# Handing the experts' output banks from TensorE to VectorE in two halves instead of one

## The chip, the core and the metric

The kernel runs on one core of a Trainium2 chip. The metric is the device time of one execution in microseconds. It is compared as the median of several runs.

## The reference

The kernel computes one hybrid block on eight images of 192 channels and 1,024 positions: a spiking convolution-attention part, causal softmax attention with six heads, and a mixture of four experts of which each token uses two. The change touches the last part alone. In the reference it is this:

```python
scores = jnp.einsum('bsd,de->bse', x, gate_w) + gate_b
probs = jax.nn.softmax(scores, axis=-1)
topk_vals, topk_idx = jax.lax.top_k(probs, TOP_K)
...
h = jax.nn.gelu(jnp.einsum('bsd,edh->ebsh', x, w1) + b1[:, None, None, :], approximate=False)
y = jnp.einsum('ebsh,ehd->ebsd', h, w2) + b2[:, None, None, :]
out = jnp.einsum('bse,ebsd->bsd', masked, y)
```

All four experts are computed for all tokens. The gate is zero where an expert isn't chosen.

## The kernel before

An image has 1,024 tokens, in two blocks of 512 (`NB = 2`), and a block has four tiles of 128 tokens (`TB = 4`). An expert's hidden layer of 768 is cut into six chunks of 128 (`HC = 6`), so a block has 24 chunks and an image 48. The order of the work on each engine is written out by hand: every engine has its own program, and semaphores join them.

For chunk `i` of an image the steps are:

- TensorE, `hidden(i)`: five matmuls of 512 columns (L437) make the chunk's hidden values in bank 0 or 1 of PSUM.
- ScalarE: GELU (L874), then the f16 high part (L882). VectorE: the f16 low part (L1330).
- TensorE, `expert_out(i - 3)` (L708): three chunks later, twelve matmuls of 192 columns, three for each of four tiles, add the chunk's share to the expert's output. Tiles 0 and 1 lie in bank 2 of PSUM and tiles 2 and 3 in bank 3. Behind the last chunk of an expert each tile gets one matmul more, for the bias (L713), and the sixteenth matmul raises `f2_done`.
- VectorE, `add_expert(y)` (L1314): once an expert is complete, four instructions multiply the four tiles by the gate and add them to `acc`. The fourth raises `y_used`.
- TensorE may write the first chunk of the next expert only when `y_used` has been raised, since there is one set of output banks.

Between these steps TensorE, ScalarE and VectorE take pieces of the next image's front part (`following`) and of this image's own tail (`aside`), at places fixed by tables (`FRONT_AT`, `TAIL_AT`). The front part ends with row maxima of the attention scores: matmuls (L596, L600) whose results VectorE reduces (L1148). The tail holds `ul` (L1192), the low part of block 1's expert input, and the front holds `al` (L1131), the same for the attention input. TensorE waits for both. The eighth image has no `following`. At the end ScalarE starts the store of `acc`, when `y_used` has its last count.

In `experts` on VectorE, `add_expert` stands ahead of the low part of chunk `i`, so that everything behind it on VectorE waits as long as it waits.

Of the kernel before, what the change touches and what calls it, by code (L numbers as in the profile page):

```python
# [10 lines left out]
ALU = mybir.AluOpType  # L11
# [4 lines left out]
B, C, N = 8, 192, 1024  # L16
# [4 lines left out]
NB = N // QB  # L21
TB = QB // P
# [5 lines left out]
EXPERTS, HID = 4, 4 * C  # L28
HC = HID // P
# [103 lines left out]
def build(nc, x_ch, x_tok, consts, w_conv, bn, w_in, w_out, b1, b2, gate_b, out):  # L133
    with ExitStack() as ctx:
        def sb(name, shape, dt):
            return ctx.enter_context(nc.sbuf_tensor(name, shape, dt))
# [3 lines left out]
        def sem(name, gain=0):  # L140
            handle = ctx.enter_context(nc.semaphore(name))
            per_image[handle.name] = gain
            return handle

        def at(s, img, n):

            return img * per_image[s.name] + n
# [38 lines left out]
        acc = sb("acc", [P, NT, C], F32)  # L186
# [23 lines left out]
        half = 4 * 2 * QB  # L210
# [48 lines left out]
        gate = sb("gate", [P, NT, EXPERTS], F32)  # L259
# [11 lines left out]
        ps = ctx.enter_context(nc.psum_tensor("ps", [P, 8, QB], F32))  # L271
# [78 lines left out]
        h_hi = sem("h_hi", NB * CHUNKS)  # L350
        h_lo = sem("h_lo", NB * CHUNKS)
        f2_done = sem("f2_done", NB * CHUNKS)
        y_used = sem("y_used", NB * EXPERTS)
        stored = sem("stored", 16 * NB)


# [71 lines left out]
        def _(pe):  # L428
            def project(dst, high, low, cols, tok, tokens_stationary):


                for n, (w, a, c) in enumerate(((win_h, high, 0), (win_l, high, 0), (win_h, low, 0),
                                               (win_t, high, 1), (win_t, low, 1))):
                    lhs, rhs = w[:, cols], a[:, c, tok]
                    if tokens_stationary:
                        lhs, rhs = rhs, lhs
                    mm = pe.matmul(dst, lhs, rhs, start=(n == 0), stop=(n == 4))  # L437
                return mm
# [234 lines left out]
            def experts(img, following):  # L673

                def hidden(i):
                    b, n = divmod(i, CHUNKS)

                    if i == 0:
                        pe.wait_ge(o_done, at(o_done, img, NB * PAIRS - 1))
                    elif i == 1:  # L680
                        pe.wait_ge(e_done, at(e_done, img, NE))
                    elif i == 3:
                        pe.wait_ge(o_done, at(o_done, img, NB * PAIRS))
                    if i >= 2:
                        pe.wait_ge(h_act, at(h_act, img, i - 1))
                    if n == 0:
                        pe.wait_ge(ul_done, at(ul_done, img, b + 1))
                    col = COL_W1 + n * P
                    project(ps[:, H_BANK[i], :], uh, ul, slice(col, col + P), slice(b * QB, (b + 1) * QB), False)\
                        .then_inc(h_ps, 1)  # L690

                def expert_out(i):
                    b, n = divmod(i, CHUNKS)
                    e, k = divmod(n, HC)
                    if k == 0:

                        if i == 0:
                            pe.wait_ge(gate_used, at(gate_used, img, 1))
                        else:
                            pe.wait_ge(y_used, at(y_used, img, i // HC))  # L700
                    pe.wait_ge(h_lo, at(h_lo, img, i + 1))
                    s = i % N_H
                    for t in range(TB):
                        dst = ps[:, 2 + t // 2, (t % 2) * C:(t % 2 + 1) * C]
                        tok = slice(t * P, (t + 1) * P)
                        for m, (hid, w) in enumerate(((h_h, wout_h), (h_h, wout_l), (h_l, wout_h))):

                            mm = pe.matmul(dst, hid[:, s, tok], w[:, n, :],  # L708
                                           start=(k == 0 and m == 0 and t % 2 == 0), stop=False,
                                           skip_group_check=True)  # L710
                        if k == HC - 1:

                            mm = pe.matmul(dst, b2_ones[:, :], b2_sb[:, e * C:(e + 1) * C],  # L713
                                           start=False, stop=True, skip_group_check=True)
                    mm.then_inc(f2_done, 1)

                aside = Aside(tail(img, 1, True))
                for i in range(NB * CHUNKS + F_LAG):
                    if i < NB * CHUNKS:
                        hidden(i)  # L720
                    following.until(i - 0.5)
                    if i >= F_LAG and (i - F_LAG) % HC == 0:

                        aside.until(i)
                        following.until(i)
                    if i >= F_LAG:
                        expert_out(i - F_LAG)
                    aside.until(i)
                    following.until(i)
                following.finish()  # L730
# [5 lines left out]
            for what, n in ((bn_t[:, 2, :], 0), (bn_t[:, 3, :], 1)):  # L736
                for p in range(3):
                    for c in range(2):
                        mm = pe.transpose(ps[0:CC + 1, p, n * C + c * CC:n * C + (c + 1) * CC],
                                          what[:, 4 * c + 1 + p:4 * c + 2 + p].broadcast_to([CC, CC + 1]),  # L740
                                          ident[0:CC, 0:CC])
# [16 lines left out]
        def _(act):  # L758
# [56 lines left out]
                rows_of_maxima(img, 0, 4)  # L815

            def store(img, b):
                act.wait_ge(y_used, at(y_used, img, (b + 1) * EXPERTS))
                act.dma_start(out[img, :, b * TB:(b + 1) * TB, :], acc[:, b * TB:(b + 1) * TB, :])\
                   .then_inc(stored, 16)  # L820

# [88 lines left out]
            for img in range(B - 1):  # L910
                experts(img, Aside(front(img + 1, True)))
                attend(img + 1, img)
            experts(B - 1, Aside(iter(())))
            store(B - 1, 1)
            act.wait_ge(stored, B * whole(stored))

# [66 lines left out]
        def _(dve):  # L983
            V = nc.vector
# [320 lines left out]
            def experts(img, following):  # L1305
                def add_expert(y):

                    b, e = divmod(y, EXPERTS)
                    dve.wait_ge(f2_done, at(f2_done, img, (y + 1) * HC))
                    for t in range(TB):  # L1310
                        n = b * TB + t
                        if y and t == 0:
                            dve.wait_ge(y_used, at(y_used, img, y))
                        ins = V.scalar_tensor_tensor(  # L1314
                            out=acc[:, n, :], in0=ps[:, 2 + t // 2, (t % 2) * C:(t % 2 + 1) * C],
                            scalar=gate[:, n, e:e + 1], in1=acc[:, n, :], op0=ALU.mult, op1=ALU.add)
                    ins.then_inc(y_used, 1)

                aside = Aside(tail(img, 1, True))
                for i in range(NB * CHUNKS + F_LAG):  # L1320
                    following.until(i - 0.5)
                    if i >= F_LAG and (i - F_LAG) % HC == HC - 1:
                        add_expert((i - F_LAG) // HC)
                    if i < NB * CHUNKS:
                        if i >= N_H:

                            dve.wait_ge(f2_done, at(f2_done, img, i - N_H + 1))
                        s = i % N_H
                        dve.wait_ge(h_hi, at(h_hi, img, i + 1))
                        V.scalar_tensor_tensor(out=h_l[:, s, :], in0=h32[:, s, :], scalar=A_SCALE,  # L1330
                                               in1=h_h[:, s, :], op0=ALU.mult, op1=ALU.subtract)\
                         .then_inc(h_lo, 1)
                    aside.until(i)
                    following.until(i)
                following.finish()
# [34 lines left out]
            for c in range(2):  # L1370
                three = wc[0:CC, c, C:].rearrange("p (k n) -> p k n", k=3)
                step(V.scalar_tensor_tensor(out=three, in0=three, scalar=W_SCALE, in1=ps[0:CC, 0:3, 0:C],
                                            op0=ALU.mult, op1=ALU.mult))
# [11 lines left out]
            for n, (kind, c0, w) in enumerate(pieces):  # L1385
# [5 lines left out]
                                       op0=ALU.mult, op1=ALU.subtract).then_inc(stage_lo, 1)  # L1391
# [79 lines left out]
```

## Time and profile before

| | before |
|---|---|
| median of 3 runs | 1701.42 us (1701.23 to 1702.93) |
| the profiled execution: its own time | 1703.11 us |
| the profiled execution: span of its instructions | 1701.1 us |
| TensorE, matmuls busy | 1590.3 us, 93% of the span |
| VectorE busy | 1188.9 us, 70% |
| ScalarE busy | 904.1 us, 53% |
| mean granted TensorE clock | 0.976 of full speed |

Busy times are sums over instructions, and the matmuls of TensorE overlap one another in them. An engine's idle time costs something only where another engine on the path to the end waits for it. The profile's names: PE is TensorE's matmul, PEld its weight load, DVE VectorE, ACT ScalarE. `L708` is line 708 of the kernel.

### The profile page before, as it was taken

How to read it: one execution, taken by the hardware profiler on the slowest of the kernel's cores; microseconds unless marked ns; L12 is line 12 of the kernel's file. 1: busy time of each engine (PE TensorE's matmuls, PEld its weight loads, DVE VectorE, ACT ScalarE, POOL GpSimd, SP SyncE). 2: the span in 40 equal slices, each digit the busy share in tenths (PEclk: the TensorE clock that was granted, in tenths of full speed). 3: DMA queues.
4: the chain of work that ended last, by engine and by line, in shares of the span. 5: the costliest groups of instructions: out<-in, count | busy, mean ns of one | idle time of the engine just before them, and what ended most of it. 6: DMA issues, size and time to landing. Idle time of an engine off the chain costs nothing.

```text
span 1701.1 us, 32601 instructions
## 1 busy us (share of the span) xinstructions
PE 1590.3 (93%) x13148; PEld 1028.3 (60%) x13148; DVE 1188.9 (70%) x2537; ACT 904.1 (53%) x1329; POOL 173.3 (10%) x247
## 2 busy tenths in 40 slices
PE   3689999999999999899998999999999999999998
PEld 1424676546665567656765567655766557665666
DVE  6685775767767676867759578576776777686643
ACT  3206654466545665456553665446654566535654
POOL 2210102001110003000120010200121000300100
PEclk9759999999999999999999999999999999999999
DMA  4112002010111002010020100201011100200000
GB/s 158 52 29 63 1 1 66 8 41 2 26 41 48 1 1 66 2 48 1 2 66 1 48 2 1 66 13 36 2 38 30 48 2 1 66 1 11 1 11 10
DMA packets 25129, 47.27 MB, mean 28 GB/s; under 512 B 7410, under 2 KB 16946, under 8 KB 23700
## 3 DMA queue, kind: packets, MB, share of 16 engines
q1 hardware_dynamic: 15728, 27.85, 5.9%
q0 software_dynamic: 6144, 9.45, 2.4%
q10 hardware_dynamic: 3108, 7.91, 1.3%
q8 instruction: 103, 1.69, 0.4%
q14 instruction: 46, 0.38, 0.1%
HBM read 19.82 MB, written 6.29 MB: 15 GB/s over the span
## 4 chain that ended last, share of the span: by engine, by line
PE 67%; DVE 23%; ACT 4%; issue 3%; POOL 1%; DMA 1%; SPq 0%; DVEq 0%; ACTq 0%; POOLq 0%
PE ps L437 20%; PE ps L708 16%; PE ps L655 10%; DVE mx L1148 7%; PE ps L472 6%; PE ps L596 3%; DVE acc L1314 3%; DVE room L1330 3%; PE ps L516 2%; DVE norm_stats L989 2%; PE ps L444 1%; PE ps L503 1%; ACT room L874 1%; PE ps L476 1%; DVE gn_st L1031 1%
## 5 line engine op out<-in xcount | busy, mean ns | idle before, releaser
L874 ACT ACTIVATE room<-ps,b_sb 128x512 f32<-128x512 f32 x384 | 263.2, 685 | 459.8 <-PE ps L437 459.8
L708 PE MATMUL ps<-wout_h,room 128*128 128x192 f16 x3072 | 459.4, 246 | 5.4 <-DVE acc L1314 5.4
L1330 DVE SCALAR_TENSOR_TENSOR room<-room 128x512 f16<-128x512 f32 x384 | 262.7, 687 | 179.2 <-ACT room L882 174.2
L708 PE MATMUL ps<-wout_l,room 128*128 128x192 f16 x1536 | 377.9, 246 | 0.0
L708 PEld LDWEIGHTS ps<-wout_h,room 128*128 128x128 f16 x3072 | 286.5, 98 | 45.7 <-DVE acc L1314 11.8
L854 ACT ACTIVATE room<-ps 128x1024 f32<-128x1024 f32 (+3 forms) x288 | 224.8, 811 | 161.0 <-PE ps L476 123.6
L1148 DVE TENSOR_REDUCE mx<-ps 128x2 f32<-128x1024 f32 (+3 forms) x288 | 265.8, 952 | 36.3 <-PE ps L600 19.2
L882 ACT ACTIVATE room<-room 128x512 f16<-128x512 f32 x384 | 241.9, 630 | 33.8 <-ACT room L874 0.4
L655 PE MATMUL ps<-room,v 128*64 128x512 f32 (+3 forms) x1152 | 232.9, 488 | 0.9 <-DVE o L1280 0.9
L596 PE MATMUL ps<-qk 96*128 96x512 f16 (+3 forms) x576 | 159.8, 349 | 38.7 <-DVE mx L1148 30.3
L708 PEld LDWEIGHTS ps<-wout_l,room 128*128 128x128 f16 x1536 | 150.4, 98 | 27.3
L472 PE MATMUL ps<-qk 98*64 98x512 f16 (+3 forms) x1152 | 157.1, 332 | 10.2 <-DVE mx L1148 7.8
L437 PE MATMUL ps<-uh,win_h 128*128 128x512 f16 x384 | 145.9, 380 | 3.0 <-DVE o L1280 3.0
L437 PE MATMUL ps<-uh,win_t 128*128 128x512 f16 x384 | 145.7, 380 | 0.0
L437 PE MATMUL ps<-ul,win_h 128*128 128x512 f16 x384 | 145.7, 379 | 0.0
L437 PE MATMUL ps<-uh,win_l 128*128 128x512 f16 x384 | 145.6, 379 | 0.0
L437 PE MATMUL ps<-ul,win_t 128*128 128x512 f16 x384 | 145.5, 379 | 0.0
L1314 DVE SCALAR_TENSOR_TENSOR acc<-ps,gate,acc 128x192 f32<-128x192 f32 x256 | 89.0, 410 | 72.4 <-PE ps L713 71.7
L472 PEld LDWEIGHTS ps<-qk 98*64 98x64 f16 x1152 | 62.2, 110 | 93.4 <-issue 47.5
L596 PEld LDWEIGHTS ps<-qk 96*128 96x128 f16 x576 | 53.7, 100 | 106.2 <-DVE mx L1148 61.5
L961 POOL TENSOR_TENSOR norm_pow<-norm_var,minus_half 128x4 f32<-128x4 f32 x16 | 18.6, 1165 | 916.7 <-DVE norm_var L1003 916.7
L655 PEld LDWEIGHTS ps<-room,v 128*64 128x64 f32 x1152 | 66.5, 137 | 30.0 <-issue 3.0
(201 smaller groups left out, 2291.0 us busy)
## 6 DMA issues: line engine op xcount, KB each, us to landing
xc<-x_ch SPq DMA_DIRECT2D x8, 768.0 KB, 5.7
qk<-qk_all SPq DMA_DIRECT2D x96, 64.0 KB, 2.4
qk<-qk_all POOLq DMA_DIRECT2D x96, 64.0 KB, 2.6
out<-acc ACTq DMA_DIRECT2D x16, 384.0 KB, 2.4
xt<-x_tok SPq DMA_DIRECT2D x7, 768.0 KB, 7.0
qk<-qk_all POOLq DMA_DIRECT2D x96, 32.0 KB, 2.0
qk<-qk_all SPq DMA_DIRECT2D x96, 32.0 KB, 2.3
room<-w_in SPq DMA_DIRECT2D x2, 1024.0 KB, 8.5
```

The costliest lines, as they stand in the source:

```text
L437: mm = pe.matmul(dst, lhs, rhs, start=(n == 0), stop=(n == 4))
L472: mm = pe.matmul(ps[keys, bank, q0:QB], k4[:, h, kc * P + keys.start:kc * P + keys.stop], q4[:, h, b * QB + q0:(b + 1) * QB], start=True, ...
L516: mm = pe.matmul(ps[:, 4 + (t + 2) % 4, 0:2 * C], xs[0:rows, c, t * P:(t + 1) * P], w[0:rows, c, C:3 * C], start=(n == 0), stop=(n == 3))
L596: mm = pe.matmul(ps[:, bank, 0:width], q4[0:3 * D, h, t * P:(t + 1) * P], k4[0:3 * D, h, half * QB:half * QB + width], start=True, stop=no ...
L655: mm = pe.matmul(ps[a * 2 * D:(a + 1) * 2 * D, bank, q0:QB], v32[:, kc * PAIRS + pair, a * D:(a + 2) * D], p32[j % N_P32][:, a, q0:QB], st ...
L708: mm = pe.matmul(dst, hid[:, s, tok], w[:, n, :], start=(k == 0 and m == 0 and t % 2 == 0), stop=False, skip_group_check=True)
L854: act.activation(p32[j % N_P32][:, :, q0:QB], ps[:, bank:bank + 2, q0:QB], ACT.Exp, scale=scale).then_inc(e_done, 1)
L874: act.activation(h32[:, i % N_H, :], ps[:, H_BANK[i], :], ACT.Gelu, scale=1 / (U_SCALE * W_SCALE), bias=b1_sb[:, n:n + 1])\
L882: act.activation(h_h[:, i % N_H, :], h32[:, i % N_H, :], ACT.Copy, scale=A_SCALE)\
L1148: V.tensor_reduce(mx[:, half, t, 2 * pair:2 * pair + 2], ps[:, bank:bank + 2, 0:width], AX.X, ALU.max)\
L1314: ins = V.scalar_tensor_tensor(out=acc[:, n, :], in0=ps[:, 2 + t // 2, (t % 2) * C:(t % 2 + 1) * C], scalar=gate[:, n, e:e + 1], in1=acc[: ...
L1330: V.scalar_tensor_tensor(out=h_l[:, s, :], in0=h32[:, s, :], scalar=A_SCALE, in1=h_h[:, s, :], op0=ALU.mult, op1=ALU.subtract)\
```

## The change

The one hand-over of four tiles becomes two of two tiles, one for each bank. TensorE raises a new semaphore `y_half` with the bias matmul of tile 1. VectorE's adds of tiles 0 and 1 wait for `y_half`, and those of tiles 2 and 3 for `f2_done`. `y_used` counts twice for an expert, and TensorE waits for it twice: before tile 0 and before tile 2 of the next expert's first chunk. The store of `acc` waits for the doubled count.

```diff
         f2_done = sem("f2_done", NB * CHUNKS)
-        y_used = sem("y_used", NB * EXPERTS)
+        y_half = sem("y_half", NB * EXPERTS)
+        y_used = sem("y_used", 2 * NB * EXPERTS)
...
                         else:
-                            pe.wait_ge(y_used, at(y_used, img, i // HC))
+                            pe.wait_ge(y_used, at(y_used, img, 2 * (i // HC) - 1))
                     pe.wait_ge(h_lo, at(h_lo, img, i + 1))
                     s = i % N_H
                     for t in range(TB):
+                        if k == 0 and i and t == TB // 2:
+                            pe.wait_ge(y_used, at(y_used, img, 2 * (i // HC)))
...
                             mm = pe.matmul(dst, b2_ones[:, :], b2_sb[:, e * C:(e + 1) * C],
                                            start=False, stop=True, skip_group_check=True)
+                            if t == TB // 2 - 1:
+                                mm.then_inc(y_half, 1)
                     mm.then_inc(f2_done, 1)
...
-                act.wait_ge(y_used, at(y_used, img, (b + 1) * EXPERTS))
+                act.wait_ge(y_used, at(y_used, img, 2 * (b + 1) * EXPERTS))
...
-                    dve.wait_ge(f2_done, at(f2_done, img, (y + 1) * HC))
-                    for t in range(TB):
-                        n = b * TB + t
-                        if y and t == 0:
-                            dve.wait_ge(y_used, at(y_used, img, y))
-                        ins = V.scalar_tensor_tensor(
-                            out=acc[:, n, :], in0=ps[:, 2 + t // 2, (t % 2) * C:(t % 2 + 1) * C],
-                            scalar=gate[:, n, e:e + 1], in1=acc[:, n, :], op0=ALU.mult, op1=ALU.add)
-                    ins.then_inc(y_used, 1)
+                    for half in range(2):
+
+                        if half == 0:
+                            dve.wait_ge(y_half, at(y_half, img, y + 1))
+                        else:
+                            dve.wait_ge(f2_done, at(f2_done, img, (y + 1) * HC))
+                        if y:
+                            dve.wait_ge(y_used, at(y_used, img, 2 * y - 1 + half))
+                        for t in range(half * TB // 2, (half + 1) * TB // 2):
+                            n = b * TB + t
+                            ins = V.scalar_tensor_tensor(
+                                out=acc[:, n, :], in0=ps[:, 2 + t // 2, (t % 2) * C:(t % 2 + 1) * C],
+                                scalar=gate[:, n, e:e + 1], in1=acc[:, n, :], op0=ALU.mult, op1=ALU.add)
+                        ins.then_inc(y_used, 1)
```

No instruction changes its place. What changes is who waits for what. On TensorE, in the eighth image, the last boundary between two experts read like this before; `b_sb,b_ones` is the bias matmul of a tile, `uh,win_h` the first matmul of `hidden`, and `room` holds the hidden values:

```order
10278 L713 MATMUL ps<-b_sb,b_ones 128x192
10279 L437 MATMUL ps<-uh,win_h 128x512 [waits h_act]
10280 L437 MATMUL ps<-uh,win_l 128x512
10281 L437 MATMUL ps<-ul,win_h 128x512
10282 L437 MATMUL ps<-uh,win_t 128x512
10283 L437 MATMUL ps<-ul,win_t 128x512
10284 L708 MATMUL ps<-wout_h,room 128x192 [waits h_lo,y_used]
10285 L708 MATMUL ps<-wout_l,room 128x192
10286 L708 MATMUL ps<-wout_h,room 128x192 x2
10287 L708 MATMUL ps<-wout_l,room 128x192
10288 L708 MATMUL ps<-wout_h,room 128x192 x2
```

At the same place TensorE's program now reads as follows (the line numbers have moved by one and by three):

```order
10333 L716 MATMUL ps<-b_sb,b_ones 128x192
10334 L438 MATMUL ps<-uh,win_h 128x512 [waits h_act]
10335 L438 MATMUL ps<-uh,win_l 128x512
10336 L438 MATMUL ps<-ul,win_h 128x512
10337 L438 MATMUL ps<-uh,win_t 128x512
10338 L438 MATMUL ps<-ul,win_t 128x512
10339 L711 MATMUL ps<-wout_h,room 128x192 [waits h_lo,y_used]
10340 L711 MATMUL ps<-wout_l,room 128x192
10341 L711 MATMUL ps<-wout_h,room 128x192 x2
10342 L711 MATMUL ps<-wout_l,room 128x192
10343 L711 MATMUL ps<-wout_h,room 128x192
10344 L711 MATMUL ps<-wout_h,room 128x192 [waits y_used]
```

Nothing stands elsewhere; a second wait for `y_used` has come between tile 1 and tile 2. On VectorE, from the second-last add to the end of the program, the order before was this (`room<-room` is the low part of a chunk):

```order
1922 L1314 SCALAR_TENSOR_TENSOR acc<-ps,gate,acc 128x192 [waits y_used,f2_done]
1923 L1314 SCALAR_TENSOR_TENSOR acc<-ps,gate,acc 128x192 x3
1924 L1330 SCALAR_TENSOR_TENSOR room<-room 128x512 [waits h_hi,f2_done] x4
1925 L1314 SCALAR_TENSOR_TENSOR acc<-ps,gate,acc 128x192 [waits y_used,f2_done]
1926 L1314 SCALAR_TENSOR_TENSOR acc<-ps,gate,acc 128x192 x3
```

And now it is this, for the same stretch of VectorE:

```order
2046 L1324 SCALAR_TENSOR_TENSOR acc<-ps,gate,acc 128x192 [waits y_used,y_half]
2047 L1324 SCALAR_TENSOR_TENSOR acc<-ps,gate,acc 128x192
2048 L1324 SCALAR_TENSOR_TENSOR acc<-ps,gate,acc 128x192 [waits y_used,f2_done]
2049 L1324 SCALAR_TENSOR_TENSOR acc<-ps,gate,acc 128x192
2050 L1340 SCALAR_TENSOR_TENSOR room<-room 128x512 [waits h_hi,f2_done] x4
2051 L1324 SCALAR_TENSOR_TENSOR acc<-ps,gate,acc 128x192 [waits y_used,y_half]
2052 L1324 SCALAR_TENSOR_TENSOR acc<-ps,gate,acc 128x192
2053 L1324 SCALAR_TENSOR_TENSOR acc<-ps,gate,acc 128x192 [waits y_used,f2_done]
```

The four adds of an expert stay together; the first now waits for `y_half`, and the third for `f2_done`.

## Rows read from the trace of the kernel before

**Rows 1.** The page: its first line, and the chain that ended last, by engine.

```profile
span 1701.1 us, 32601 instructions
...
PE 67%; DVE 23%; ACT 4%; issue 3%; POOL 1%; DMA 1%; SPq 0%; DVEq 0%; ACTq 0%; POOLq 0%
```

**Rows 2.** Waits, whole span: who waited for whom, us in total, times, longest.

```profile
DVE acc L1314 <- PE ps L713: 71.7, 43, 3.1
...
PEld ps L472 <- issue: 47.5, 186, 0.8
...
PEld ps L596 <- issue: 18.5, 30, 1.4
...
PEld ps L708 <- DVE acc L1314: 11.8, 13, 1.0
...
PE ps L708 <- DVE acc L1314: 5.4, 13, 0.5
```

**Rows 3.** Timeline, fourth image, around its fifth expert: start us, duration us.

```profile
879.74 0.25 PE L713 MATMUL ps<-b_sb,b_ones 128*128 128x192 f16 x1
...
880.40 0.25 PE L713 MATMUL ps<-b_sb,b_ones 128*128 128x192 f16 x1
...
880.69 1.39 DVE L1314 SCALAR_TENSOR_TENSOR acc<-ps,gate,acc 128x192 f32<-128x192 f32 x4 [2.84 <-PE ps L713]
...
881.35 0.38 PE L437 MATMUL ps<-ul,win_t 128*128 128x512 f16 x1
...
882.00 0.68 DVE L1330 SCALAR_TENSOR_TENSOR room<-room 128x512 f16<-128x512 f32 x1
...
882.14 0.26 PE L708 MATMUL ps<-wout_h,room 128*128 128x192 f16 x1 [0.41 <-DVE acc L1314]
```

**Rows 4.** Timeline, eighth image: from one chunk's hidden values to the next expert_out.

```profile
1663.53 0.38 PE L437 MATMUL ps<-ul,win_t 128*128 128x512 f16 x1
...
1663.75 0.25 PE L708 MATMUL ps<-wout_h,room 128*128 128x192 f16 x1
```

**Rows 5.** Timeline, eighth image, the adds of the last expert.

```profile
1696.97 1.39 DVE L1314 SCALAR_TENSOR_TENSOR acc<-ps,gate,acc 128x192 f32<-128x192 f32 x4 [2.09 <-PE ps L713]
```

**Rows 6.** Timeline, fourth image, from its first expert to the gate scores.

```profile
800.34 0.69 DVE L1330 SCALAR_TENSOR_TENSOR room<-room 128x512 f16<-128x512 f32 x1
...
800.78 0.25 PE L713 MATMUL ps<-b_sb,b_ones 128*128 128x192 f16 x1
...
801.73 1.39 DVE L1314 SCALAR_TENSOR_TENSOR acc<-ps,gate,acc 128x192 f32<-128x192 f32 x4 [0.69 <-PE ps L713]
...
804.15 1.00 ACT L826 ACTIVATE uh<-ps 128x1024 f16<-128x1024 f32 x1
...
805.57 1.21 DVE L1192 SCALAR_TENSOR_TENSOR ul<-ps,uh 128x1024 f16<-128x1024 f32 x1
...
806.46 0.25 PE L708 MATMUL ps<-wout_h,room 128*128 128x192 f16 x1
...
806.84 0.18 PE L437 MATMUL ps<-win_h,uh 128*128 128x4 f16 x1
```

**Rows 7.** Line 1192 (`ul`), all instructions: who waited for it, us, times.

```profile
  PEld ps L437: 2.5, 7
```

**Rows 8.** Timeline, fourth image, around its fourth expert.

```profile
858.01 1.39 DVE L1314 SCALAR_TENSOR_TENSOR acc<-ps,gate,acc 128x192 f32<-128x192 f32 x4 [1.02 <-PE ps L713]
...
860.83 0.38 PE L437 MATMUL ps<-al,win_t 128*128 128x512 f16 x1
...
861.19 0.39 PE L437 MATMUL ps<-ah,win_h 128*128 128x512 f16 x1
```

**Rows 9.** Timeline, fourth image, VectorE in the row maxima.

```profile
894.46 3.07 DVE L1148 TENSOR_REDUCE mx<-ps 128x2 f32<-128x768 f32 x3
897.62 1.39 DVE L1314 SCALAR_TENSOR_TENSOR acc<-ps,gate,acc 128x192 f32<-128x192 f32 x4
...
921.36 1.38 DVE L1314 SCALAR_TENSOR_TENSOR acc<-ps,gate,acc 128x192 f32<-128x192 f32 x4
```

## The prediction

> **What bounds the kernel now.** I read the page first: the span is 1701.1 us, and the chain of work that ended last runs over TensorE for 67% of it and over VectorE for 23% [rows 1]. So I ask where TensorE stands still and who ends it. That is the list of waits. Its two rows on the changed lines say that the first matmul of an expert's first chunk (L708) stood still for the adds (L1314) 13 times, and no more [rows 2]. An image has seven boundaries between experts, eight images have 56; the other 43 are covered by front or tail work. The other direction is longer: VectorE sat idle for the end of an expert 43 times, 71.7 us in all [rows 2]. That costs something only where TensorE later waits for what stands behind the adds on VectorE. So I went through one whole image on the timeline, with its TensorE gaps, and then saw that the other images have the same ones.
>
> The kind of stop to see first is at the fifth expert [rows 3]. The last bias matmul starts at 880.40, VectorE begins the four adds at 880.69, `hidden` is through with its last start at 881.35, and the next expert's first matmul starts only at 882.14. Six of the 13 stops are of the eighth image, which has no front work to cover them, one is in each of the other seven.
>
> **The change part by part.** Lengths first. Four adds take 1.39 us, and the instruction behind them starts 1.31 us after the first [rows 3]: one add holds VectorE for 0.33 us and its result is there after 0.41. From a bias matmul's start to the first add's start is 0.29 us (880.40 to 880.69), and from the end of the adds (882.08) to the matmul that waited is 0.06. The bias matmul of tile 1 stands 0.66 us ahead of that of tile 3 (879.74, 880.40) [rows 3]. So `y_half` lets the adds of tiles 0 and 1 start up to 0.66 us sooner, they take 0.66 us, and the adds of tiles 2 and 3 then go at the old start of all four. VectorE is free 0.65 us sooner wherever it had been idle long enough.
>
> (1) The 13 stops. Without one, the matmul would start 0.22 us behind the last of `hidden` (1663.53 to 1663.75, where nothing is waited for [rows 4]), at 881.57; it starts at 882.14, so a stop costs 0.57 us. After the change tiles 0 and 1 are added from 880.03 to 880.77 and released at 880.83, 0.74 us before TensorE wants bank 2. Tiles 2 and 3 are added from 880.69 to 881.43, released at 881.49; TensorE wants bank 3 six matmuls of 0.08 us after 881.57, at 882.07. Both are in time with over half a microsecond to spare, so the stop goes whole: 13 x 0.57 = 7.4 us. What TensorE does behind it depends on TensorE's own earlier work, and the row maxima that come next begin at TensorE's pace, so I keep all of it.
>
> (2) The end. Behind the last expert there are only the adds and the store. The adds start at 1696.97 and take 1.39 us [rows 5]; two of them are now done by then, so 0.65 us goes.
>
> (3) `ul`. At the first expert VectorE had been idle for 0.69 us before 801.73. The low part ahead of it starts at 800.34 and holds VectorE until about 801.0; `y_half` comes at 800.78 + 0.29 = 801.07. So the adds end 0.65 us sooner. Behind them VectorE is busy without a gap until `ul` at 805.57, whose other input is there at 804.15 + 1.00 = 805.15. `ul` moves ahead to about 805.18, 0.39 us. TensorE had its last matmul of `expert_out` at 806.46 and could go on at 806.54, but started at 806.84 [rows 6]: 0.30 us lost, all of it returned. There are seven such waits [rows 7]: 7 x 0.30 = 2.1 us.
>
> (4) `al`. At the fourth expert VectorE was idle for 1.02 us, so again it is 0.65 us ahead. `al` comes two instructions behind, and TensorE's matmul that needs it starts at 861.19 where 860.83 + 0.22 = 861.05 was possible [rows 8]: 0.14 us, in seven images 1.0 us.
>
> (5) The sixth expert, in the row maxima, where VectorE is what TensorE waits for. Three reductions start at 894.46 and are 3.07 us long; with the overlap of 0.08 VectorE is free at 897.45, and the adds start at 897.62, when `f2_done` has come [rows 9]. `y_half` has come by then, so 0.17 us goes; in seven images 1.2 us. The third, and the seventh at 921.36 [rows 9], are not waited for: their matmuls are through before VectorE is free. Nothing there.
>
> What is added: 64 increments and 56 waits on TensorE, 128 waits on VectorE, almost all already met when reached. The matmul at 1663.53 raises a semaphore and the one at 1663.75 waits for one that was raised long before, and the gap is what it is inside a row of such matmuls [rows 4]. On VectorE, the low part behind the adds waits for two semaphores and starts 0.33 us behind the last add, as an add behind an add does [rows 3]. So I put all of them at nothing. The bounds: on TensorE from nothing to 0.62 us for a wait, the mean time in which weight loads stood for no cause that is shown (18.5 us, 30 times), with the commoner one at 0.26 us (47.5 us, 186 times) [rows 2]. On VectorE at most the lost overlap of 0.08 us, which counts only at the third, sixth and seventh expert: 21 x 0.08 = 1.7 us. I take nothing for both, since the nearest rows are those of these same lines.
>
> A page speaks against the free increments. The Trainium skill, "TensorE: Matmul & The Clock Gate", section "The cost: per-tile semaphore tail", says that completion increments of TensorE's matmuls queue up behind one another, at 26.3 ns each. By it 64 more increments would be an estimated 1.7 us, and the time 1690.7 us. The row above shows no delay behind an increment, and the page's own case is many increments at once.
>
> The sum: 7.4 + 0.65 + 2.1 + 1.0 + 1.2 = 12.4 us. Made against the profiled execution this is a span of 1688.7 us. Its own time was 1703.11 us, 1.7 us above the median of the runs, 1701.42; from the median it is 1689.0 us, which I predict. That is 0.7% faster; about 0.2%, 3.4 us, can be told from no change.
>
> **The rivals.** The likeliest, as worked out: 1689.0 us, its own range 1687 to 1691.5, chance 0.65. In it the DVE bound of 1.7 us and the smallest items may go either way.
>
> Only the direct stops go. Items (3) to (5) are short waits with three engines close together; if ScalarE's or POOL's work ends them instead, 8.05 us are left and the time is 1693.4 us. For it: `ul`'s other input comes only 0.42 us before `ul` starts. Against it: each of them has its own room in the rows. Chance 0.17.
>
> VectorE's earlier end is worth more. If all 43 waits were on the path, 43 x 0.65 = 28 us would go, 1673 us. Against it: most of them have TensorE running beyond with no gap. Chance 0.05, and more likely just a few microseconds below my number.
>
> The change does what it says, but takes back as much: if the wait ahead of tile 2 cost TensorE 0.26 us each of 56 times, because the weight load behind it isn't drawn ahead, that is 14.6 us, and the time is 1703.6 us, no change. For it: in the attention part loads stand just so. Against it: the first load of `expert_out` has a wait too and doesn't. Chance 0.08.
>
> The same mechanism at its upper bound ends slower: at 0.62 us it is 34.7 us, 1723.7 us. It decides from (12.4 + 3.4) / 56 = 0.28 us for one. Chance 0.05.
>
> **How the numbers follow.** Likeliest and "only the direct stops" hold 0.82; from 1685.5 to 1694.5 both are inside, with the low side of the third for a few microseconds more. Faster by over 0.2%: 0.65 + 0.17 + 0.05 = 0.87. Within: 0.08. Slower: 0.05.
>
> **What would show it.** In the list of waits the two rows of L708 on the adds (13 times) should be gone, also in the eighth image, and an expert there should take 0.57 us less from one set of adds to the next. VectorE's wait before the adds should shrink by about 0.6 us each. TensorE's wait for `ul` should be gone and that for `al` much shorter. A gap of TensorE between tile 1 and tile 2 of a first chunk would be the two last rivals. If the first halves don't start 0.29 us behind tile 1's bias matmul, `y_half` doesn't come when I think. I would be wrong above all if a wait that is met still costs TensorE its load ahead, or if the time won in (1) were lost again before the image ends.

## The result, and the profile after

| kernel | median us | runs | against before (95%) |
|---|---|---|---|
| before, on the same chip | 1703.43 | 1701.23 to 1704.33 (6) | 1 |
| changed | 1693.01 | 1692.25 to 1697.42 (6) | 0.9948 [0.9934, 0.9962] |

The changed kernel is 0.52% faster by the ratio of all runs; the two medians lie 10.4 us apart. On the 1701.42 us that the prediction started from, the ratio's interval is 6.5 to 11.2 us less. The median is 4.0 us above the predicted 1689.0. Of this, 2.0 us are the starting level: 1701.42 us was the median of three runs of before, and with three more it is 1703.43. The profiled execution took 1692.58 us, with a span of 1690.7: 10.4 us less than before's.

First the page of the changed kernel, its first line and the chain that ended last, beside [rows 1].

```profile
span 1690.7 us, 32657 instructions
...
PE 70%; DVE 20%; ACT 4%; issue 3%; POOL 1%; DMA 1%; SPq 0%; DVEq 0%; ACTq 0%; POOLq 0%
```

VectorE's share of the chain is smaller (23% to 20%). The list of waits of the changed kernel (who <- whom: us, times, longest) says where it went.

```profile
DVE acc L1324 <- PE ps L716: 43.3, 33, 2.4
...
PEld ps L438 <- DVE al L1136: 1.1, 1, 1.1
```

The adds waited 43 times and 71.7 us [rows 2], and now 33 times and 43.3 us. The two rows of TensorE waiting for the adds are gone, and so is that for `ul` [rows 7]. The fifth expert of the fourth image, on the timeline of the changed kernel (start, duration), answers to [rows 3].

```profile
873.27 0.25 PE L716 MATMUL ps<-b_sb,b_ones 128*128 128x192 f16 x1
873.36 0.25 PE L711 MATMUL ps<-wout_h,room 128*128 128x192 f16 x1
...
873.56 1.40 DVE L1324 SCALAR_TENSOR_TENSOR acc<-ps,gate,acc 128x192 f32<-128x192 f32 x4 [2.18 <-PE ps L716]
...
873.93 0.25 PE L716 MATMUL ps<-b_sb,b_ones 128*128 128x192 f16 x1
...
874.88 0.38 PE L438 MATMUL ps<-ul,win_t 128*128 128x512 f16 x1
...
875.10 0.25 PE L711 MATMUL ps<-wout_h,room 128*128 128x192 f16 x1
```

Tile 1's bias matmul at 873.27 raises `y_half`, and the adds start at 873.56, 0.29 us behind. The adds of tiles 2 and 3 go straight on: two adds after 873.56 is 874.22, just when `f2_done` comes (873.93 + 0.29). The next expert's first matmul starts 0.22 us behind the last of `hidden`, where before it started 0.79 us behind. And 873.27 to 873.36 is the step of every such matmul: the increment costs TensorE nothing there.

Three of the small waits and the end, again the timeline of the changed kernel, beside [rows 6, 8, 9] and [rows 5].

```profile
798.22 1.01 ACT L831 ACTIVATE uh<-ps 128x1024 f16<-128x1024 f32 x1
799.26 1.22 DVE L1197 SCALAR_TENSOR_TENSOR ul<-ps,uh 128x1024 f16<-128x1024 f32 x1
...
800.52 0.25 PE L711 MATMUL ps<-wout_h,room 128*128 128x192 f16 x1
800.61 0.17 PE L438 MATMUL ps<-win_h,uh 128*128 128x4 f16 x1
...
854.52 0.38 PE L438 MATMUL ps<-al,win_t 128*128 128x512 f16 x1
854.73 0.38 PE L438 MATMUL ps<-ah,win_h 128*128 128x512 f16 x1
...
887.41 3.06 DVE L1153 TENSOR_REDUCE mx<-ps 128x2 f32<-128x768 f32 x3
890.39 0.73 DVE L1324 SCALAR_TENSOR_TENSOR acc<-ps,gate,acc 128x192 f32<-128x192 f32 x2
...
1686.52 1.40 DVE L1324 SCALAR_TENSOR_TENSOR acc<-ps,gate,acc 128x192 f32<-128x192 f32 x4 [1.43 <-PE ps L716]
1686.89 0.25 PE L716 MATMUL ps<-b_sb,b_ones 128*128 128x192 f16 x1
```

`ul` starts as soon as `uh` is there, and TensorE goes on 0.09 us behind `expert_out` (before: 0.38). `al` is in time (0.21 us from start to start, before 0.36). The sixth expert's adds follow the reductions with the usual overlap, and the last adds start 0.37 us ahead of tile 3's bias matmul.

So every stop is gone, but the sum of these places is more than 10.4 us (12.4 in the prediction). I set the starts of each image's first adds side by side (the next image's less this one's):

| | first adds | images 1 to 7 | eighth image, first adds to end |
|---|---|---|---|
| before | 196.16 | 202.97, 201.29, 201.31, 201.29, 201.31, 201.30, 200.41 | 95.06 |
| changed | 195.21 | 199.98, 199.98, 199.97, 199.98, 201.65, 201.64, 200.76 | 91.53 |

A like image is 1.32 us shorter (201.30 to 199.98; the seventh has less front work behind it). But one image of before and three of the changed kernel are 1.67 us longer than their like: 202.97, and 201.65, 201.64 and 200.76. The view of windows shows what those have (us, then busy time and count of PE, PEld, DVE, ACT and POOL, then granted TensorE clock, DMA share, GB/s), here for the same place in the changed kernel's fourth and fifth images:

```profile
914.00:924.00 10.00, 8.26 (x58) 4.73 (x55) 9.38 (x14) 3.10 (x5) 0.00 (x0) 1.00 0.01 2
1114.00:1124.00 10.00, 8.27 (x49) 4.99 (x48) 7.72 (x13) 2.63 (x4) 0.00 (x0) 0.83 0.01 2
```

PE is as busy in both, with fewer matmuls in the second (x49), at a mean granted clock of 0.83. That is 3.4 us at half, the 1.2 GHz level, and 1.7 us lost. TensorE's own timeline of the fifth image shows where:

```profile
1117.00 0.34 PE L597 MATMUL ps<-qk 96*128 96x384 f16 x1 [1.49 <-DVE mx L1153]
...
1118.31 0.25 PE L711 MATMUL ps<-wout_h,room 128*128 128x192 f16 x1
...
1120.02 0.63 PE L438 MATMUL ps<-uh,win_h 128*128 128x512 f16 x1
1120.45 0.63 PE L438 MATMUL ps<-uh,win_l 128*128 128x512 f16 x1
...
1122.48 0.25 PE L711 MATMUL ps<-wout_h,room 128*128 128x192 f16 x1
```

TensorE stood 1.49 us for a row maximum, behind the seventh expert. From about 1118.5 its matmuls take 0.63 us and follow at 0.43 where they had taken 0.38 and followed at 0.22, and by 1122.48 it is over. I call this a clock fall. Beyond the start-up, before has one in its profile (from 320) and the changed kernel three (from 1118, 1319 and 1521). This is before's, in its first image, behind the same wait (its window, then TensorE's timeline):

```profile
316.00:326.00 10.00, 8.26 (x49) 4.97 (x48) 7.72 (x12) 2.63 (x4) 0.00 (x0) 0.83 0.01 2
...
318.70 0.34 PE L596 MATMUL ps<-qk 96*128 96x384 f16 x1 [1.49 <-DVE mx L1148]
```

The 1.49 us wait itself stands in all seven images in both kernels. Another wait for a row maximum, behind the sixth expert, did change: it is item (5) of the prediction. First before, then the changed kernel, in the fourth image:

```profile
900.90 0.59 PE L596 MATMUL ps<-qk 96*128 96x512 f16 x2 [1.13 <-DVE mx L1148]
```

```profile
893.65 0.59 PE L597 MATMUL ps<-qk 96*128 96x512 f16 x2 [0.94 <-DVE mx L1153]
```

This accounts for the span. The first adds come 0.95 us sooner: 0.65 because `y_half` is earlier, 0.30 in the start-up. Since all the adds stand 0.65 us earlier against TensorE, this 0.65 is the one that is won at the end, item (2), and it counts once. The 0.30 is nothing that the change does: between executions of the changed kernel alone the first adds differ by more (195.21 here, 198.06 in after_again below). Seven images give 7 x 1.32 = 9.2, and the eighth 3.5 (95.06 to 91.53). Two clock falls more take back 3.3. Together 10.4 us; without clock falls on either side it would be 13.7.

### The profile page after: what moved, and what is told of

Read it like the earlier page. It is cut to its first block, busy times and chain, and to the rows that moved or that the text cites. A ratio compares the mean times of both kernels' runs of the same rounds, so it can differ in the third digit from the quotient of the medians.

```text
span 1690.7 us, 32657 instructions
## 1 busy us (share of the span) xinstructions
PE 1588.7 (94%) x13148; PEld 1033.0 (61%) x13148; DVE 1189.7 (70%) x2537; ACT 904.3 (53%) x1329; POOL 173.5 (10%) x247
## 4 chain that ended last, share of the span: by engine, by line
PE 70%; DVE 20%; ACT 4%; issue 3%; POOL 1%; DMA 1%; SPq 0%; DVEq 0%; ACTq 0%; POOLq 0%
PE ps L438 22%; PE ps L711 17%; PE ps L656 10%; DVE mx L1153 7%; PE ps L473 6%; PE ps L597 3%; PE ps L517 2%; DVE room L1340 2%; PE ps L445 2%; DVE acc L1324 2%; DVE norm_stats L994 2%; PE ps L504 1%; ACT room L879 1%; PE ps L477 1%; DVE gn_st L1036 1%
## 5 line engine op out<-in xcount | busy, mean ns | idle before, releaser
L1324 DVE SCALAR_TENSOR_TENSOR acc<-ps,gate,acc 128x192 f32<-128x192 f32 x256 | 89.3, 411 | 43.8 <-PE ps L716 43.3
```

The source lines that it names most:

```text
L1324: ins = V.scalar_tensor_tensor(out=acc[:, n, :], in0=ps[:, 2 + t // 2, (t % 2) * C:(t % 2 + 1) * C], scalar=gate[:, n, e:e + 1], in1=acc[: ...
```

## The experiments

All stand against before on the same chip; the medians of before were 1703.77, 1703.59 and 1702.95 us in the three sets. "Falls" are those of the profiled execution after its start-up.

| kernel | median us (runs) | ratio (95%) | falls | like image |
|---|---|---|---|---|
| early_start | 1693.04 (5) | 0.9939 [0.9927, 0.9952] | 3 | 199.98 |
| early_release | 1700.33 (10) | 0.9978 [0.9969, 0.9987] | 3 | 200.79 |
| after_fill | 1689.68 (4) | 0.9918 [0.9904, 0.9931] | 0 | 199.98 |
| after_again | 1696.16 (5) | 0.9950 [0.9936, 0.9964] | 5 | 199.98 |
| before_fill | 1703.98 (11) | 0.9999 [0.9990, 1.0008] | 1 | 201.27 |
| fill_sixth | 1696.57 (5) | 0.9956 [0.9943, 0.9968] | 3 | 200.44 |
| fill_start | 1683.78 (4) | 0.9885 [0.9869, 0.9900] | 0 | 199.98 |
| fill_again | 1689.59 (4) | 0.9914 [0.9901, 0.9928] | 0 | 199.98 |
| longer_image | 1698.97 (7) | 0.9974 [0.9964, 0.9985] | 1 | 201.27 |
| fill_half | 1688.22 (4) | 0.9910 [0.9894, 0.9925] | 0 | 199.98 |

**early_start: VectorE starts early, but TensorE waits for both halves.**

```diff
-                            pe.wait_ge(y_used, at(y_used, img, 2 * (i // HC) - 1))
+                            pe.wait_ge(y_used, at(y_used, img, 2 * (i // HC)))
...
-                        if k == 0 and i and t == TB // 2:
-                            pe.wait_ge(y_used, at(y_used, img, 2 * (i // HC)))
```

> VectorE starts tiles 0 and 1 at y_half as in the changed kernel, but TensorE waits for all four tiles before tile 0 of the next expert, as before. Theory one: the early start alone carries the whole gain, since the four adds then end 0.08 us before TensorE wants them; the list of waits has no stop of L708 for the adds, one image takes 199.98 us from one first set of adds to the next wherever the clock is full (before 201.30), and the time is that of the changed kernel, 1693 us, within 1.5 us. Rival: the release in halves is what removes the stops; then all 13 stops of 0.57 us are back, 7.4 us, and the time is about 1700 us. Stretches of 3.4 us at half clock come on top of either, 1.7 us each.

It is as fast as the changed kernel (1693.04 and 1693.01 us), with the same images. Its timeline at the fifth expert:

```profile
874.20 1.40 DVE L1322 SCALAR_TENSOR_TENSOR acc<-ps,gate,acc 128x192 f32<-128x192 f32 x4 [2.18 <-PE ps L714]
...
875.52 0.38 PE L438 MATMUL ps<-ul,win_t 128*128 128x512 f16 x1
875.66 0.10 PEld L709 LDWEIGHTS ps<-wout_h,room 128*128 128x128 f16 x1 [0.25 <-DVE acc L1322]
875.74 0.25 PE L709 MATMUL ps<-wout_h,room 128*128 128x192 f16 x1
```

The adds are through at 875.60, and the weight load goes 0.06 us later. The matmul behind it still starts 0.22 us after 875.52, so the load's wait lies under the running matmul. The wait ahead of tile 2 is not needed for the gain, and with it in place (the changed kernel) it costs nothing either.

**early_release: the reverse, banks released in halves, but VectorE waits for all four tiles.**

```diff
-                            if t == TB // 2 - 1:
-                                mm.then_inc(y_half, 1)
...
-                            dve.wait_ge(y_half, at(y_half, img, y + 1))
+                            dve.wait_ge(f2_done, at(f2_done, img, (y + 1) * HC))
```

> VectorE waits for f2_done for all four tiles, as before, but raises y_used after two and after four, and TensorE waits for it before tile 0 and before tile 2. Theory one: the first half is released at 881.49 on the clock of the trace before, 0.08 us before TensorE wants it, the second at 882.14, 0.07 us after TensorE wants it, so a stop shrinks from 0.57 to about 0.07 us and 13 of them give 6.5 us; items (2) to (5), 0.65 + 2.1 + 1.0 + 1.2 us and the 0.9 us by which they measured larger, stay away. One image takes 200.8 us where the clock is full, and with one to three stretches at half clock the time is 1695 to 1699 us. Rival: the split of the release is worth the whole gain, and the time is 1693 us.

Its list of waits, and the timeline at the fifth expert:

```profile
DVE acc L1321 <- PE ps L715: 72.1, 43, 3.1
...
PEld ps L710 <- DVE acc L1321: 3.5, 14, 0.3
...
PEld ps L437 <- DVE ul L1194: 2.5, 7, 0.4
```

```profile
881.24 1.39 DVE L1321 SCALAR_TENSOR_TENSOR acc<-ps,gate,acc 128x192 f32<-128x192 f32 x4 [2.84 <-PE ps L715]
...
882.03 0.10 PEld L710 LDWEIGHTS ps<-wout_h,room 128*128 128x128 f16 x1 [0.25 <-DVE acc L1321]
882.12 0.25 PE L710 MATMUL ps<-wout_h,room 128*128 128x192 f16 x1
```

VectorE waits as before (43 times, 72.1 us; before 71.7), and TensorE's wait for `ul` is back, 2.5 us in seven. The direct stop is nearly gone all the same: a like image is 0.5 us shorter than before's 201.30, and the eighth image's experts, 13.33 us apart before, are 12.83 apart against the changed kernel's 12.75. So either half of the change removes the direct stops, and items (2) to (5) need the early start. The time is 1.3 us above the upper end of what I expected. The image's length (200.79 for the expected 200.8) and the falls (three for one to three) came as expected; but the sum started from 1701.42 us, and before stands at 1703.77 in this set. One of the three falls, in the first image, is behind the sixth expert, where this kernel's wait is 1.12 us as in before.

**after_fill: 20 matmuls that nobody reads, in the 1.49 us wait of seven images.** They go to spare columns of a bank of PSUM, ahead of the score product that waits, and start when the seventh expert's adds are through. Edit on the changed kernel, N_KEEP being 20:

```diff
+                    if later and i == 29:
+                        pe.wait_ge(y_used, at(y_used, img - 1, 14))
+                        for n in range(N_KEEP):
+                            pe.matmul(ps[:, 3, 2 * C:QB], wout_h[:, 0, 0:P], wout_h[:, 1, 0:P],
+                                      start=False, stop=True, skip_group_check=True)
```

> The changed kernel, and in the seven images with front work 20 matmuls of 128 columns, whose results nobody reads, in the time in which TensorE waits for the reductions after the seventh expert's adds (idle 1.49 us there). Theory one: the stretches of 3.4 us at half clock come after that wait, three of them in the profiled execution, and take back 1.7 us each; with the wait filled they are gone, every image takes 199.98 us, and the time is 1686 to 1689 us, with less spread than the changed kernel's 1692.3 to 1697.4. Rival: the falls of the clock have nothing to do with this wait; they stay, and the time is 1693 us, or 1 to 2 us more for the filler.

Its timeline in the fourth image, then its windows for the fifth:

```profile
916.39 1.29 PE L590 MATMUL ps<-wout_h 128*128 128x128 f16 x20
...
917.85 0.34 PE L603 MATMUL ps<-qk 96*128 96x384 f16 x1 [0.18 <-DVE mx L1159]
```

```profile
1114.00:1124.00 10.00, 9.55 (x82) 6.17 (x80) 9.39 (x14) 2.63 (x4) 0.00 (x0) 1.00 0.00 0
```

The unread matmuls stand inside the wait, the images are 199.98 us, all seven, and there is no fall. The ratio is 0.9918 where the changed kernel had 0.9948, and 1689.68 us is 0.7 us above the upper end of what I expected.

**after_again: the changed kernel, unchanged, on the chip of after_fill.**

> The changed kernel once more, unchanged, to see in a second profile how many images have a stretch at half clock. Theory one: images without one take 199.98 us again, to 0.05 us, images with one take 201.65 us, and the time of an execution is 1685.6 us plus the start-up's variation plus 1.7 us for each. Rival: the images lose their time in another way, and the lengths lie between the two.

The ratio is 0.9950, beside 0.9948 the first time. Its profiled execution took 1698.80 us, 6.2 us more than that of the first, and has five falls instead of three, in images three to seven. Its windows for the fourth image, where the first profile had 1.00:

```profile
918.00:928.00 10.00, 8.26 (x52) 4.89 (x50) 7.72 (x12) 2.42 (x4) 0.00 (x0) 0.83 0.01 2
```

Two falls more are 3.4 us; the rest of the 6.2 is the start-up (first adds at 198.06 in place of 195.21). So the number of falls differs between executions of one program, and with the start-up it spreads its times (1692.31 to 1698.80 us); after_fill's four lie within 3.6 us. In the three profiles of an image of 199.98 us with its wait unfilled (the changed kernel's two and early_start) the falls begin in some image, the fifth, the third and the fifth, and then come in every image up to the seventh.

**before_fill: the same filler in the kernel before** (`img - 1, 7` in the wait, since it counts whole experts there).

> The kernel before, with the same 20 unread matmuls in the same wait after the seventh expert's adds. Theory one: the kernel before loses 1.7 us to the clock in one image or so out of seven, and the filler takes that away; every image takes 201.30 us, the time is about 1701.5 us, and against the filled changed kernel the difference is that of the items alone, 1.32 us for each of seven images, 3.5 us in the eighth and 0.65 us at the end, 13.4 us. Rival: the filler helps the kernel before as much as the changed one, 3 to 6 us, and the difference stays near 10 us.

No difference to before: 0.9999. I had expected an execution without a fall. None comes behind the seventh expert, whose wait is filled, but one comes behind the sixth, whose wait is 1.12 us in this kernel:

```profile
1103.43 0.59 PE L602 MATMUL ps<-qk 96*128 96x512 f16 x2 [1.12 <-DVE mx L1154]
...
1105.40 0.37 PE L714 MATMUL ps<-wout_l,room 128*128 128x192 f16 x1
```

The image with it is 1.35 us longer than its like (202.63 and 201.28), where before's single fall cost 1.67. The filler thus gives before nothing that can be told, and the changed kernel about 5 us. Medians of fill_again and before_fill in one set are 14.4 us apart; seven images, the eighth and the 0.65 us of the earlier adds, without falls, give 13.4.

**fill_sixth: the same filler at another wait**, the 0.94 us one behind the sixth expert (`i == 11`, `img - 1, 12`). The expectation calls this wait 1.1 us, which it is in before.

> The changed kernel with the 20 unread matmuls in another wait, that of 1.1 us after the sixth expert's adds. Theory one: the falls of the clock belong to the wait after the seventh; they stay, some images take 201.65 us, and the time is 1692 to 1697 us. Rival: any 1.2 us of work more in the stage of the row maxima is enough; then no image takes more than 200 us and the time is 1686 to 1690 us.

It does not help: three falls, each behind the seventh expert's 1.49 us wait. Its timeline:

```profile
919.46 0.34 PE L603 MATMUL ps<-qk 96*128 96x384 f16 x1 [1.49 <-DVE mx L1159]
...
921.21 0.36 PE L717 MATMUL ps<-wout_l,room 128*128 128x192 f16 x1
```

The score product ends the wait at 919.46, and by 921.21 a matmul of 0.25 us takes 0.36. The place of the filler matters, not that there is some. It also made a like image 0.46 us longer: 20 of these matmuls take 1.29 us, more than this wait has.

**longer_image: 23 unread matmuls, but where TensorE is busy,** so that an image is as long as before's.

```diff
+                    if img < B - 1 and i == 25:
+                        for n in range(23):
+                            pe.matmul(ps[:, 3, 2 * C:QB], wout_h[:, 0, 0:P], wout_h[:, 1, 0:P],
+                                      start=False, stop=True, skip_group_check=True)
```

> The changed kernel with 23 unread matmuls of 128 columns in each of the first seven images at a place where TensorE is busy without a gap (behind the second chunk of the fifth expert), so that an image without a stretch at half clock takes about 201.3 us, as in the kernel before; the waits in the row maxima are untouched. Theory one, now open on this point: when a fall comes depends on how the waits of 1.49 us lie against something of the chip that is not in the program, so the length of an image decides how many images have one; with the old length they become as rare as before (one in two profiles of the kernel before), and the time is that of the kernel before less the eighth image's 3.5 us and the end's 0.65 us: about 1699 us. Rival: something in the changed kernel's own row maxima brings the falls; then three to five images have one again (203 us each), and the time is 1702 to 1706 us.

The waits are those of the changed kernel, the 0.94 and the 1.49 us ones, but the falls are as in before: one, in the first image. Its windows for the first and the second:

```profile
316.00:326.00 10.00, 8.26 (x52) 5.14 (x51) 8.02 (x12) 1.87 (x4) 0.00 (x0) 0.83 0.01 2
517.00:527.00 10.00, 8.26 (x62) 5.02 (x60) 9.68 (x13) 2.63 (x4) 0.00 (x0) 1.00 0.00 0
```

So neither of these waits is new or longer in the changed kernel. That its extra falls go with its shorter image fits this, but it rests on one profile, and the 23 matmuls also add work to TensorE in each image; nothing here takes these two apart.

**fill_half: after_fill with N_KEEP = 10.**

> The filled changed kernel with 10 unread matmuls in place of 20 after the seventh expert, 0.65 us of the wait of 1.49. Theory one: it is the length without matmuls that counts; with about 0.8 us left, less than the 0.94 us after the sixth expert that brought no fall in the changed kernel, there are no falls: seven images of 199.98 us, 1687 to 1691 us. Rival: half the filler is too little, some images take 201.65 us, and the time is 1691 to 1697 us.

Ten are enough in its profile: no fall, 1688.22 us. **fill_again**, after_fill once more, gave 1689.59.

> The filled changed kernel once more. Theory one: again no stretch at half clock after the start in any image, seven images of 199.98 us, and a time of 1687 to 1691 us. Rival: the first profile had none by chance, and one or more images take 201.65 us.

**fill_start: after_fill, and six unread matmuls ahead of each pair of score products of the first image, from the third pair on.** The start-up had long stretches at half clock in every profile.

```diff
+                    if not later and i >= 2:
+                        for n in range(6):
+                            pe.matmul(ps[:, 3, 2 * C:QB], win_h[:, 0:P], win_h[:, P:2 * P],
+                                      start=True, stop=True, skip_group_check=True)
```

> The filled changed kernel, and in the first image six unread matmuls ahead of each wait of TensorE for the reductions of the row maxima, where the clock is at half from 84 to 133 us and 23.9 us of full clock are lost. Theory one: TensorE has too little to do there for the full clock; with the filler it comes back before the first image's attention starts (118 us), and the part up to the first image's first adds is 3 to 8 us shorter: 1680 to 1685 us. Rival: the clock stays down until the attention's own matmuls bring it up, and the filler only gets in the way at half clock, plus 0 to 3 us.

Windows of the changed kernel, then of fill_start, for the same stretches of the start-up:

```profile
88.00:118.00 30.00, 24.96 (x93) 8.28 (x91) 25.29 (x30) 1.87 (x2) 0.97 (x2) 0.50 0.08 20
118.00:133.00 15.00, 12.69 (x67) 4.94 (x68) 7.98 (x10) 3.29 (x5) 0.00 (x0) 0.53 0.01 1
```

```profile
88.00:118.00 30.00, 26.25 (x288) 18.27 (x285) 27.99 (x33) 1.87 (x2) 1.71 (x4) 1.00 0.10 27
118.00:133.00 15.00, 12.92 (x134) 6.93 (x131) 7.99 (x15) 8.29 (x11) 0.00 (x0) 0.89 0.01 2
```

The granted clock is 1.00 where it was 0.50, and the first adds come at 189.87 where fill_again had 195.97. At 1683.78 us this is the best version: 1.15% faster than before, more than twice the gain of the change.

## Why the prediction was right or wrong

**What bounds it** was right: TensorE and the places where it stands still. All 13 direct stops went.

**(1)** A stop was put at 0.57 us; the eighth image's experts are 0.58 us closer (13.33 to 12.75). Right.

**(2)** The end was put at 0.65. The last adds now start 0.37 us ahead of tile 3's bias matmul instead of 0.29 behind, 0.66. Right.

**(3) to (5)** were put at 0.30, 0.14 and 0.17 an image, and with the stop at 1.18; measured was 1.32. `ul` returned its 0.30, `al` 0.15 (0.36 to 0.21), and the sixth expert 0.19 (its wait went from 1.13 to 0.94). The rest, about 0.1 us, comes in steps of a few hundredths, the largest near 831 us of before's trace; no run follows them up. In seven images the 0.14 us above the 1.18 make 1.0 of the 1.3 us that came in above the sum; the start-up's 0.30 is the other part.

**The free waits** are right. An image has the length that follows from the stops alone, which leaves no room for 0.26 or 0.62 us at each of 56 waits, the two last rivals. early_start, which lacks the wait ahead of tile 2, has the same image to 0.01 us. The estimate made with the 26.3 ns of the Trainium skill, "TensorE: Matmul & The Clock Gate", section "The cost: per-tile semaphore tail", does not show here, where the increments come one at a time: 873.27 to 873.36 is the usual step. The 1693.4 us of "only the direct stops go" lies near the median, but its mechanism did not happen: (3) to (5) all came in. So it is luck that 1693.01 us lies inside 1685.5 to 1694.5: it is above 1691.5, the end of the range of the account that was held likeliest, and what put it there is in none of the rivals. The last sign named, time won in (1) lost again before the image ends, comes nearest: the images with a fall take 201.65 us, 0.35 more than a like image of before.

**The step that failed** is the one in (1): "What TensorE does behind it depends on TensorE's own earlier work, and the row maxima that come next begin at TensorE's pace, so I keep all of it." The stops did go whole, but the sum had no term for the TensorE clock, which it put at nothing without a reason. Before's trace had such a place, one fall of 1.7 us from 320, and I had not looked at the granted clock by stretches. Two falls more in the profile took back 3.3 us (four more in after_again, 6.7), against 1.3 us that came in above the sum: 12.4 + 1.3 - 3.3 = 10.4. The other half of the 4.0 us is before's own level, 1703.43 for 1701.42. That the falls are the missing term is shown by taking them away in their place only: after_fill 0.9918, fill_again 0.9914, fill_half 0.9910, where fill_sixth (0.9956) did nothing. The predicted ratio was 1689.0 / 1701.42 = 0.9927.

In the changed kernel every fall follows the longest wait that TensorE has in that part of the image, and ten short matmuls in that wait avoid it. Where VectorE does not start early and the wait behind the sixth expert is 1.12 us, a fall came behind that one too (once in early_release, once in before_fill); where it is 0.94 us, none did in any profile. The Trainium skill, "TensorE: Matmul & The Clock Gate", section "HAM oscillation — how this bites in real kernels", tells of a TensorE that is set back to the lower clock by its waits over and over. The trace agrees that a wait can do it, with 1.7 us lost each time, but the waits told of there are for DMA, 3 to 5 us long, and do it in every pass; here 1.49 us did it, in some images only. What stays open is why the same 1.49 us wait is followed by a fall in some images and not in others: three of seven in one execution, five in another, one in before and in longer_image. The length of the image may play a part (199.98 against 201.27 us, with the waits alike); this is argued from one profile of longer_image and not shown. What on the chip decides it was not worked out.

## What to carry to other kernels

Where a consumer stands idle for the end of a group of tiles, give it the first bank as soon as that is whole: here the early start carries the gain, and the release in halves adds nothing once the adds start early. Count a removed stall at full length only after a look at the granted clock by stretches, in before's trace too, for a shorter loop may meet the lower clock more often. Where TensorE falls to the lower clock behind a wait, some unread matmuls inside that wait, and not elsewhere, can keep it up: they gave 5 us here beside the change, and 6 us more in the start-up.

## What I had not expected of the hardware

The front part of the first image runs at half clock for 45 us (granted clock 0.50 in 88 to 118, 0.53 in 118 to 133), with PE busy for over four fifths of the time. Six unread matmuls ahead of each pair of score products (93 matmuls in the first stretch, then 288) held that stretch at 1.00.

Beyond the start-up, every fall in these profiles has one length, 3.4 us at half clock: 0.83 over 10 us. Behind the seventh expert one costs 1.7 us; the two behind the sixth cost less (1.36 us in early_release, 202.15 against 200.79, and 1.35 in before_fill). And one program has three of them in one execution and five in another.
